# One kernel of four transformer layers: a norm of a norm in one stage, layer 2's weight loads inside the norm before it, and two attention loops written out

## The reference

```python
xn = _layernorm(x)                    # eps 1e-5, no scale, no bias
x = x + attn_ref(xn, ...) + ffn_ref(xn, ...)
```

```python
x = _ln(inputs, ln1_scale, ln1_bias)               # layer 1 attention, eps 1e-6, inputs = xn
attn_out = layer_norm(residual, attn_nw, attn_nb)  # layer 3 experts, eps 1e-12, residual = xn
```

## Time and profile before

| what | us |
|---|---|
| median of 3 runs | 2138.48 (2133.2 to 2142.51) |
| the profiled execution, its own time | 2138.84 |
| its span in the trace | 2135.9 |

### The profile page before, as it was taken

One profiled execution on the slowest core, in us unless ns is written; L12 is line 12 of the kernel. 1 busy time (PEld: TensorE's weight loads), 2 busy tenths in 40 slices (PEclk: granted clock), 3 DMA queues, 4 the chain that ended last, 5 costly groups with the idle time before them and its releaser, 6 DMA issues. The chain is left out here.

```text
span 2135.9 us, 31634 instructions
## 1 busy us (share of the span) xinstructions
PE 1751.4 (82%) x10687; PEld 1129.4 (53%) x10687; DVE 1415.0 (66%) x2084; ACT 1224.6 (57%) x2064; POOL 1135.8 (53%) x1025
## 2 busy tenths in 40 slices
PE   4737999999487477676888999899999899999958
PEld 1514777789343266443453555555555555555535
DVE  3465777763355487665238888888888888888831
ACT  4274333346246266234337877777777777777733
POOL 1154545524100366211323788888888788878860
PEclk9578999997699799797899999999999999999979
DMA  1212222221000000000413999999899998899970
GB/s 28 64 36 72 80 80 80 79 62 34 14 18 1 6 0 0 3 4 22 127 46 61 156 165 156 162 158 158 158 156 157 157 160 158 155 163 161 161 134 20
DMA packets 630961, 193.01 MB, mean 90 GB/s; under 512 B 591553, under 2 KB 622034, under 8 KB 630814
## 3 DMA queue, kind: packets, MB, share of 16 engines
q1 hardware_dynamic: 621686, 167.32, 43.4%
q0 software_dynamic: 8224, 23.51, 3.6%
q10 hardware_dynamic: 904, 0.29, 0.1%
HBM read 36.90 MB, written 12.48 MB: 23 GB/s over the span
## 5 line engine op out<-in xcount | busy, mean ns | idle before, releaser
L2833 DVE TENSOR_REDUCE half_max<-scores 128x1 f32<-128x1024 f32 x512 | 614.7, 1219 | 142.3 <-PE scores L2662 136.5
L2579 POOL TENSOR_TENSOR p_low<-p,p_high 128x2048 f16<-128x2048 f32 (+15 forms) x256 | 576.4, 2252 | 153.2 <-ACT p_high L2763 131.4
L2662 PE MATMUL scores<-k_high,q_pair 128*128 128x512 f16 x1024 | 304.1, 378 | 68.1 <-ACT p L2748 63.1
L2748 ACT ACTIVATE p<-scores,exp_bias 128x1024 f32<-128x1024 f32 (+7 forms) x384 | 317.7, 862 | 64.8 <-DVE exp_bias L2838 62.3
L2763 ACT ACTIVATE p_high<-p 128x2048 f16<-128x2048 f32 (+15 forms) x256 | 282.5, 1104 | 40.8 <-DMA pT_high<-p_high 34.1
L2662 PE MATMUL scores<-k_low,q_pair 128*128 128x512 f16 x1024 | 304.7, 379 | 0.0
L2682 PEld LDWEIGHTS scores<-v_pair,pT_high 128*128 128x128 f16 x2176 | 151.2, 99 | 108.9 <-issue 57.5
L2682 PE MATMUL scores<-v_pair,pT_low 128*128 128x129 f16 x2176 | 187.3, 223 | 15.2 <-DMA pT_low<-p_low 14.6
L2682 PE MATMUL scores<-v_pair,pT_high 128*128 128x129 f16 x2176 | 188.8, 222 | 8.5 <-DMA pT_high<-p_high 8.4
L2682 PEld LDWEIGHTS scores<-v_pair,pT_low 128*128 128x128 f16 x2176 | 147.3, 99 | 53.1 <-DMA pT_low<-p_low 21.9
L2662 PEld LDWEIGHTS scores<-k_low,q_pair 128*128 128x128 f16 x1024 | 99.3, 97 | 122.0 <-issue 0.5
(11 more groups left out here) (486 smaller groups left out, 3272.2 us busy)
## 6 DMA issues: line engine op xcount, KB each, us to landing
pT_high<-p_high SPq DMA_TRANSPOSE x256, 3.7
pT_low<-p_low SPq DMA_TRANSPOSE x256, 3.7
slots<-zero_row SPq DMA_DIRECT2D x1, 3036.0 KB, 14.3
slot_rows<-slots SPq DMA_DIRECT2D x23, 132.0 KB, 2.4
slots_out<-expert_out SPq DMA_DIRECT2D x23, 128.0 KB, 1.8
w_up<-in_L_ffn_inter_w_dram SPq DMA_DIRECT2D x1, 2048.0 KB, 9.3
dispatched<-moe_rows SPq DMA_DIRECT2D x1, 1024.0 KB
slot_rows<-dispatched SPq DMA_DIRECT2D x4, 256.0 KB, 4.0
```

The costliest lines, as they stand in the source:

```text
L2579: pool.tensor_tensor(flat(pl[:, buf, b0:b0 + n, :]), flat(p32[:, buf, b0:b0 + n, :]), flat(ph[:, buf, b0:b0 + n, :]), ALU.subtract).then_i ...
L2662: mm = pe.matmul(ps[:, b.start + i, :], q, k[:, par, cs(2 * half + i)], start=start, stop=not start)
L2748: act.activation(flat(p32[:, buf, b0 + first:b0 + first + w, :]), flat(ps[:, banks(p, half), :])[:, 0:w * P], ACT.Exp, bias=bias[:, p:p + ...
L2833: dve.tensor_reduce(mx[:, p % 2, half:half + 1], flat(ps[:, b[half], :]), AX.X, ALU.max, negate=True)\
```

## The change

`layernorm` gets an argument `again`. With it the stage makes both norms from the one centred input and the one variance. The variance of a norm's result is v / (v + eps), and the product of the two inverse roots is one root of another sum: 1 / sqrt(v (1 + eps2) + eps eps2). So per chunk ACT takes a second Ln and a second Exp from the same `ln_var`, and DVE does a second multiply and the scale and bias. The second call of `layernorm` goes in both places, and its loads move into the fused stage.

The four `load_all` stages of layer 2 go. Their 12 transfers become `loads` of the norm in front of the layer, all issued by SP. The tiles they fill are allocated before that norm and live through the layer.

`steps` in `l2_window` and `l2_latent` writes all 32 and 16 steps out.

```diff
-def layernorm(nc, m, src, dst, eps, width=P, scale=None, bias=None, after=None, loads=()):
+def layernorm(nc, m, src, dst, eps, width=P, scale=None, bias=None, after=None, loads=(), again=None):
...
-                act.wait_ge(eps_set, 1)
+                act.wait_ge(eps_set, 1 if again is None else 2)
...
                     act.activation(work[w, cs(c)], work[w, cs(c)], ACT.Exp, scale=-0.5).then_inc(inverted, 1)
+                    if again is not None:
+                        act.activation(work2[w, cs(c)], var[w, c, :], ACT.Ln, bias=epst2[w, :], scale=1.0 + eps2)\
+                           .then_inc(logged_again, 1)
+                        act.wait_ge(logged_again, c + 1)
+                        act.activation(work2[w, cs(c)], work2[w, cs(c)], ACT.Exp, scale=-0.5).then_inc(inverted_again, 1)
...
+                    if again is not None:
+                        dve.wait_ge(inverted_again, c + 1)
+                        dve.tensor_tensor(dst2[w, cs(c)], cen[w, cs(c)], work2[w, cs(c)], ALU.mult).then_inc(normed_again, 1)
+                        dve.wait_ge(normed_again, c + 1)
+                        dve.tensor_scalar(dst2[w, cs(c)], dst2[w, cs(c)], scale2, bias2, ALU.mult, ALU.add)\
+                           .then_inc(scaled_again, 1)
...
-        layernorm(nc, m, m.xn, y, 1e-12, scale=m.col("L3_ffn_attn_nw"), bias=m.col("L3_ffn_attn_nb"),
+        layernorm(nc, m, m.x, m.xn, LN_EPS, again=(y, 1e-12, m.col("L3_ffn_attn_nw"), m.col("L3_ffn_attn_nb")),
...
-        layernorm(nc, m, m.xn, y, 1e-6, scale=m.col("L1_attn_ln1_scale"), bias=m.col("L1_attn_ln1_bias"), loads=loads)
+        layernorm(nc, m, m.x, m.xn, LN_EPS, loads=loads,
+                  again=(y, 1e-6, m.col("L1_attn_ln1_scale"), m.col("L1_attn_ln1_bias")))
...
-        load_all(nc, [(wv[:], inp["L2_attn_wv"])])
...
             def steps(eng, body):
 
-                for s in range(4):
-                    body(s, s)
-                with eng.Fori(1, STEPS // 4 - 1) as i:
-                    for k in range(4):
-                        body(i * 4 + k, k)
-                for k in range(4):
-                    body(STEPS - 4 + k, k)
+                for s in range(STEPS):
+                    body(s, s % 4)
...
+        r.wv, r.wg = sb("w_v", [P, P]), sb("w_latent", [P, 4, LAT])
+        layernorm(nc, m, m.x, m.xn, LN_EPS,
+                  loads=[(w[:, 0, :], inp["L2_attn_wq"]), (w[:, 1, :], inp["L2_attn_wk"]), (w[:, 2, :], inp["L2_attn_w_out"]),
+                         (wr[:], inp["L2_attn_r_out_w"]), (r.wv[:], inp["L2_attn_wv"]),
+                         (r.wg[:, 0, :], inp["L2_attn_wgq"]), (r.wg[:, 1, :], inp["L2_attn_wgq"]),
+                         (r.wg[:, 2, :], inp["L2_attn_wgk"]), (r.wg[:, 3, :], inp["L2_attn_wgv"])]
+                  + [(w_ffn[:, i, :], inp["L2_ffn_W_" + n]) for i, n in enumerate("rkv")])
```

More of the change, by code:

```diff
@@ L247, in layernorm @@
         epst = own.enter_context(sbuf(nc, "ln_eps", [P, 1]))
+        if again is not None:
+            dst2, eps2, scale2, bias2 = again
+            work2 = own.enter_context(sbuf(nc, "ln_work_again", [P, TOK]))
+            epst2 = own.enter_context(sbuf(nc, "ln_eps_again", [P, 1]))
         with stage(nc, "eps_set", "mean_ready", "centered", "squared", "var_ready", "logged", "inverted", "normed",
-                   "scaled", "activated", "loaded") as (
+                   "scaled", "activated", "loaded", "logged_again", "inverted_again", "normed_again", "scaled_again") as (
                 block, eps_set, mean_ready, centered, squared, var_ready, logged, inverted, normed, scaled, activated,
-                loaded):
+                loaded, logged_again, inverted_again, normed_again, scaled_again):
             @block.sync
@@ L288, in _ @@
                 dve.memset(epst[:], eps).then_inc(eps_set, 1)
+                if again is not None:
+                    dve.memset(epst2[:], eps * eps2).then_inc(eps_set, 1)
                 for c in range(NCH):
@@ L1757, in layer1_attention, with layer2_ffn @@
         hidden_mlp_and_units(nc, m, w, y, xres)
-def layer2_ffn(nc, m, inp):
+def layer2_ffn(nc, m, w):
     with ExitStack() as own:
         sb = lambda name, shape: own.enter_context(sbuf(nc, name, shape))
-        w, wt = sb("w_rkv", [P, 3, P]), sb("w_rkv_T", [P, 3, P])
+        wt = sb("w_rkv_T", [P, 3, P])
         om = sb("one_less_mu", [P, 2])
@@ L1767, in layer2_ffn @@
         rr, kk = sb("r_gate", [P, TOK]), sb("k_act", [P, TOK])
-        load_all(nc, [(w[:, 0, :], inp["L2_ffn_W_r"]), (w[:, 1, :], inp["L2_ffn_W_k"]), (w[:, 2, :], inp["L2_ffn_W_v"])])
         wps = own.enter_context(psum(nc, "w_turned", [P, CH]))
@@ L1854, in l2_window @@
         mask0 = sb("first_mask", [P, 2, KW])
-        wv = sb("w_v", [P, P])
+        wv = r.wv
         qm = sb("q_masked", [P, 2, 2, 4, WIN])
@@ L2094, in l2_latent @@
         sb = lambda name, shape: own.enter_context(sbuf(nc, name, shape))
-        wg = sb("w_latent", [P, 4, LD])
+        wg = r.wg
         pool2 = sb("pooled", [P, 2, NL])
@@ L2104, in l2_latent @@
         pm = sb("pooled_mean", [P, NL])
-        load_all(nc, [(wg[:, 0, :], inp["L2_attn_wgq"]), (wg[:, 1, :], inp["L2_attn_wgq"]),
-                      (wg[:, 2, :], inp["L2_attn_wgk"]), (wg[:, 3, :], inp["L2_attn_wgv"])])
         cps = own.enter_context(psum(nc, "latent_const", [P, CH]))
@@ L2118, in steps @@
             def steps(eng, body):
-                for n in range(4):
-                    body(n, n)
-                with eng.Fori(1, NT // 4 - 1) as i:
-                    for k in range(4):
-                        body(i * 4 + k, k)
-                for k in range(4):
-                    body(NT - 4 + k, k)
+                for n in range(NT):
+                    body(n, n % 4)
             G8 = [P, LH, NL]
@@ L2295, in _, with layer2, layer2_attention @@
                 back(NT - 1, 1)
-def layer2_attention(nc, m, inp):
+def layer2(nc, m, inp):
+    with sbuf(nc, "w_rkv", [P, 3, P]) as w_ffn:
+        layer2_attention(nc, m, inp, w_ffn)
+        layer2_ffn(nc, m, w_ffn)
+def layer2_attention(nc, m, inp, w_ffn):
     with ExitStack() as own:
@@ L2305, in layer2_attention @@
         gate_w = sb("gate_blocks", [P, 2, P])
-        load_all(nc, [(w[:, 0, :], inp["L2_attn_wq"]), (w[:, 1, :], inp["L2_attn_wk"]), (w[:, 2, :], inp["L2_attn_w_out"]),
-                      (wr[:], inp["L2_attn_r_out_w"])])
+        r.wv, r.wg = sb("w_v", [P, P]), sb("w_latent", [P, 4, LAT])
[5 more added lines that the diff above has]
+                  + [(w_ffn[:, i, :], inp["L2_ffn_W_" + n]) for i, n in enumerate("rkv")])
         with ExitStack() as inner:
@@ L2923, in build @@
         turn_in(nc, m)
-        for branches in ((layer0,), (layer1_attention,), (layer2_attention, layer2_ffn)):
-            layernorm(nc, m, m.x, m.xn, LN_EPS)
-            for branch in branches:
-                branch(nc, m, inp)
+        layernorm(nc, m, m.x, m.xn, LN_EPS)
+        for branch in (layer0, layer1_attention, layer2):
+            branch(nc, m, inp)
         r = Named()
```

## The result

| | before | changed |
|---|---|---|
| median, us | 2138.85 (4 runs, 2133.2 to 2142.51) | 2104.06 (4 runs, 2101.35 to 2108.64) |
| span of the profiled execution, us | 2135.9 | 2102.4 |
| ratio, 95% interval | | 0.9849 [0.9828, 0.9871] |

The change makes the kernel 34.8 us faster, where I had said 30.8 against the profiled run. A second batch of five runs of the changed kernel gave 2108.56, 31.6 under the kernel before beside it. Over all nine the median is 2106.4.

The account below looks back on a forecast made before the run. Short stages behind barriers, each paced by one dependent chain, were taken to bound the changed part, so whole stage lengths count. Norms 8.24 + 8.90, load stages 12.82 and loops 0.7 gave 30.7 us off 2138.8: 2108 us, range 2100 to 2117.

Parts of the forecast that it names:

- Fused norms: Layers 1 and 3: second norm stages go, ACT's second Ln and Exp pairs come in; gains 8.24 and 8.90 us.
- Load stages: Layer 2: four load stages go, each worth its length from first issue to first work; gain 12.82 us.
- Loads at nothing: Layer 2's norm: 12 moved loads take 7.8 us under 10.7 of norm, so cost nothing, at most 0.2.
- Loops: Layer 2's window and latents: writing out steps saves 0.09 us a turn, 0.7 us in all; bounds nothing and 1.5.
- rival of fetch stalls: Written-out steps of window and latents wait for instruction fetch, 2.3 us each, 74 us in all: 2182 us; chance 0.02.
- PE's clock: Restarts after idle PE run at 1.2 GHz; changes taken as zero net, with 2 us either way for all restarts.
- More than the stages: Rival: fewer slow PE restarts behind three of four load stages, up to 2 us each, 6 more: 2102 us; chance 0.05.
- the two restarts: k and v behind layer 1's fused norm lose up to 0.8 us; layer 2's projections get up to 0.8 back.
- Layer 3's attention: Left alone by the diff; the prediction falls if it takes more than 5 us longer or less than before.
- The sum: Whole kernel: 8.24 + 8.90 + 12.82 + 0.7 = 30.7 us gained, giving 2108 us.

Follow-up runs that it names:

- the doubled loads: The changed kernel with twelve more loads, to a spare tile, ahead of the twelve in layer 2's norm: 2107.45 us, ratio 0.9855.
- with loops: The changed kernel with both attentions of layer 2 back in loops over groups of four steps: 2105.04 us, ratio 0.9846.
- without: The changed kernel, all steps written out, with one empty stage ahead of the latent attention: 2104.03 us, ratio 0.9844.
- both kernels with busy norms: The changed kernel with matmuls nobody reads in three norms: eight in each, 2102.91 us; or 8, 3 and 4 in layers 1, 2 and 3, 2100.15 us.
- busy heads: The changed kernel with matmuls nobody reads at the heads of layer 2's attentions, 13 in the window, 5 and 2 in the latents: 2104.43 us.
- before again: The kernel before, unchanged, run once more for a second profile: 2149.5 us, one run.
- changed again: The changed kernel, unaltered, timed again for a second profile: 2108.56 us over 5 runs, ratio 0.9855 against the kernel before.
- the third part alone: The kernel before with only the steps of layer 2's two attentions written out: 2133.01 us, ratio 0.9964.
- Loads only: The kernel before with only layer 2's 12 loads moved into its norm and the four load stages gone: 2120.18 us, ratio 0.9904.
- empty stages: The kernel before with the 12 loads moved into layer 2's norm and an empty stage where each load stage was: 2124.64 us, ratio 0.9926.

## Why the prediction was right

*Fused norms*, 8.24 and 8.90: measured 8.22 and 8.88. The sum of the earlier trace rows held term by term: pairs 1.24 apart, DVE keeping up, 0.80 us from the last scale and bias to the next stage.

*Load stages*, 12.82: all four went. Layer 2's norm with the load behind it lost 3.59 (said 3.67), the gates with theirs 3.21 (3.26); nothing else differs there. In q and k and at the window's end I subtract the load's own 2.78 and 3.11 of the earlier trace rows from 3.98 and 5.60, and the 1.2 and 2.5 left I put down to the clock. At the window's end the slow matmuls above show it. In q and k the granted clock over the stage's first 10 us does, before and then in the changed kernel:

```profile
705.49:715.49 10.00, 9.81 (x16) 3.97 (x16) 2.71 (x6) 2.39 (x4) 0.00 (x0) 0.73 0.00 0
```

```profile
699.05:709.05 10.00, 8.62 (x16) 3.57 (x16) 3.25 (x6) 2.39 (x4) 0.00 (x0) 0.85 0.00 0
```

Twice what is missing from 1.0 is 5.4 and 3.0 us at half speed, and 2.4 us less of it is worth 1.2.

*Loads at nothing*: right, and the doubled loads put a price beyond the cover, 2.93 us where the sum 24 x 0.46 + 2.3 against 10.7 gave 2.6.

*Loops*, 0.7: half of what the profile shows. The window gains 1.45 us and the latents 0.16 where their clock stays up (78.01 with loops, 77.85 without): 1.6. What failed is the row I took as written out: two steps at the end of the old loop (7.26 us) still carried the tail of it; the same two take 7.19 in the changed kernel. Really written out, four steps take 14.38 and not 14.52. The rival of fetch stalls fell: no step waits, and PE's fetches grew by 4 packets. What the Trainium skill ("Runtime: NRT & Kernel Launch", Instruction fetch mechanics) says of a taken branch out of the window of held instructions did not bite either: a turn back costs 0.23 us, a tenth of a transfer's 2.3. Whether these loop bodies leave that window no run shows.

*PE's clock*, zero with 2 either way: the net is small, the parts are not, and that they nearly cancel was luck. In the first pair of profiles it costs 2.8 in the latents, 1.7 in the norm behind layer 1's attention, 0.5 at k and v and 1.4 in the units (granted 0.93 on average over that stage for 0.95, some 2 us more at half speed, so about 1 us of the 1.4 is the clock and the rest stays open); it gives back 2.5 at the window's end, 1.2 at its start and 1.2 at q and k. Together 1.5 us of loss. So the rival *More than the stages* came for the most part, 4.9 of its 6 us, and places that no rival named took 6.4 back. I had looked only at the two restarts I could name, and had their signs right. What PE does in the fused norm reaches further than its own next stage: with PE kept busy in it, the norm three stages on goes back from 13.8 to 12.1, in both kernels with busy norms, while all seven profiles that leave the fused norm idle have 13.8. Whether the idle time does this by itself, or because k and v end 0.8 us sooner and all behind them starts sooner, the runs don't separate. The Trainium skill ("TensorE: Matmul & The Clock Gate", Part 1: The HAM clock gate) makes activity what lifts the clock; these two kernels agree (granted 1.00 for 0.74 over q and k), while the one with busy heads had its clock up early in the latents and lost it all the same, behind 2.8 us of waiting. The same section says that the chip's watch on activity runs freely, so that one kernel meets a different number of slow matmuls at its start from run to run. The two profiles of before have such a difference in the middle of the kernel (latents 78.26 and 81.15 us).

*Layer 3's attention*: I had set 5 us as the bound, and it moved by 4.9 in the first pair of profiles. The second pair has 1031.78 and 1030.89. Over all fourteen profiles it lies between 1027.80 and 1035.12, with the same instructions in all, so the 4.9 says nothing about the change.

*The sum*: 17.1 + 12.7 + 1.6 - 1.5 = 29.9 us by stages, against 30.7 said. That is the first pair of profiles, whose stages lose 29.7. The second pair, before again and changed again, loses 36.2 in the same stages, since that profile of before is slower in k and v, layer 1's attention and the latents. So the stages priced from their lengths are sure, and the clock's share of the whole is known to 6.5 us only. The measured 34.8, or 31.6 in the second batch, has the variation of layer 0 and layer 3's attention on it. How much of the 8 us of the third part alone, and of the excess in the sum of the parts, is of that kind stays open.

## What to carry to other kernels

Where short stages follow each other behind barriers, cut the trace at the first work of each stage and price a change by stage lengths; four terms of 3 to 9 us came out within 0.1. Then look at PE's granted clock in the stages behind, untouched ones too: removing or fusing work moves where it falls, by 1 to 3 us a place and in both signs, and only repeated profiles tell which of it belongs to the change. Where PE idles through the tail of a stage, a few matmuls on data that is there anyway, and no more than fit, speed up the next start (q and k took 8.53 us for 10.05). Whether the kernel gains by it shows only in the sum over all stages: here 4.5 us were won and 4.2 lost in others.

## What I had not expected of the hardware

- The clock fell from 2.4 back to 1.2 GHz within 5 us of having risen, behind only 2.0 us without a matmul (859.86 to 862.26), and in other runs of like code it did not, behind 2.3 us.
- Two profiles of the same program gave stage lengths that differ by 1.6 to 2.9 us in three places (k and v, layer 1's attention, latents). Loads only and empty stages, whose instructions are the same up to there, differ alike (k and v 20.83 and 18.94). Two profiles of the changed kernel agreed within 0.1 in every stage from layer 1's norm to the experts.
- A stage with nothing in it costs 0.77 us.
- A turn of a four-engine hardware loop costs 0.23 us, in the first two steps behind the turn.
